# The products q·att of a linear attention as eight 64-row products in two row groups, instead of four 128-row products with zero blocks

## The reference

```python
xn = ln(x)
q = softmax((xn @ Wq + bq).reshape(b, t, h, 64), axis=-1)
k = softmax((xn @ Wk + bk + (1 - mask) * -1e6).reshape(b, t, h, 64), axis=1)
v = ((xn @ Wv + bv) * mask).reshape(b, t, h, 64)
att = einsum('bnhd,bnhl->bhdl', k, v)               # a 64 x 64 block for each head
y = einsum('bnhd,bhdl->bnhl', q, att)               # the products changed here
hh = ln(y) * (1 + scale) + shift                    # scale, shift from silu(emb) @ W_emb
out = x + silu(hh) @ W_out + b_out
```

## Time and profile before

| | us |
|---|---|
| median of 3 runs (510.15, 510.24, 513.07) | 510.24 |
| the profiled execution, its own time | 512.37 |
| its span in the profile | 510.5 |
| PE busy in the span | 471.0 |
| DVE busy | 365.2 |
| ACT busy | 264.6 |

### The profile page before, as it was taken

The page is one execution under the profiler, slowest core; times in us unless marked ns, Lnnn a source line. Parts: engine busy times, 40 slices in busy tenths (PEclk is TensorE's granted clock), DMA queues, the critical chain, the costliest instruction groups (busy, mean ns, idle before and its releaser), DMA issues.

```text
span 510.5 us, 7297 instructions
## 1 busy us (share of the span) xinstructions
PE 471.0 (92%) x2478; PEld 374.1 (73%) x2478; DVE 365.2 (72%) x893; ACT 264.6 (52%) x487; POOL 125.4 (25%) x106
## 2 busy tenths in 40 slices
PE   4998999999899989999999999998799979888987
PEld 2676776876688678878888888886578667676765
DVE  6699776686878747888685676759968348776643
ACT  4243333232787322355566555648898217366773
POOL 0013311120100001013343222344111201544655
PEclk9999999999999989999999999998999999999989
DMA  8991111111222211011121213211320001322444
GB/s 286 362 342 42 42 41 38 47 40 64 82 84 88 78 42 40 4 42 62 42 83 42 83 43 124 74 52 50 115 105 0 1 1 62 111 97 84 124 152 137
DMA packets 23093, 43.50 MB, mean 85 GB/s; under 512 B 1992, under 2 KB 2064, under 8 KB 23056
## 3 DMA queue, kind: packets, MB, share of 16 engines
q1 hardware_dynamic: 21968, 40.93, 23.8%
q10 hardware_dynamic: 1088, 2.10, 1.2%
HBM read 34.64 MB, written 8.39 MB: 84 GB/s over the span
## 4 chain that ended last, share of the span: by engine, by line
PE 69%; DVE 17%; ACT 6%; issue 5%; DMA 1%; POOL 0%; DVEq 0%; ACTq 0%
PE ps L1053 18%; PE ps L1055 17%; PE ps L1054 17%; PE ps L1058 8%; PE ps L1215 4%; PE ps L1146 1%; DVE xst_raw L611 1%; ACT ps L394 1%; DVE kf L810 1%; DVE qs L710 1%; DVE yst_raw L611 1%; ACT x_in L308 1%; DVE qmax L715 1%; DVE kf L746 1%; ACT kf L382 1%
## 5 line engine op out<-in xcount | busy, mean ns | idle before, releaser
L559 POOL TENSOR_TENSOR qs<-qs,qmax 128x512 f32<-128x512 f32 x32 | 35.2, 1099 | 203.1 <-DVE qmax L715 203.1
L1053 PE MATMUL ps<-wk_hi,zT_hi 128*128 128x512 f32 x128 | 54.3, 424 | 2.3 <-DVE kf L696 2.2
L1053 PE MATMUL ps<-ek_hi,zm_hi 128*128 128x512 f32 x128 | 50.8, 397 | 4.4 <-DVE ek_lo L751 3.7
L1053 PE MATMUL ps<-wq_hi,zT_hi 128*128 128x512 f32 x128 | 52.6, 411 | 0.3 <-DVE qs L710 0.3
L1054 PE MATMUL ps<-wk_lo,zT_hi 128*128 128x512 f32 x128 | 51.3, 401 | 0.0
L1055 PE MATMUL ps<-wk_hi,zT_lo 128*128 128x512 f32 x128 | 51.2, 400 | 0.0
L1055 PE MATMUL ps<-wq_hi,zT_lo 128*128 128x512 f32 x128 | 50.6, 395 | 0.0
L1054 PE MATMUL ps<-wq_lo,zT_hi 128*128 128x512 f32 x128 | 50.5, 395 | 0.0
L1055 PE MATMUL ps<-ek_hi,zm_lo 128*128 128x512 f32 x128 | 49.9, 390 | 0.0
L1054 PE MATMUL ps<-ek_lo,zm_hi 128*128 128x512 f32 x128 | 49.9, 390 | 0.0
L572 POOL TENSOR_TENSOR res<-res,bo_all 128x512 f32<-128x512 f32 x32 | 41.9, 1311 | 32.3 <-PE ps L1055 19.9
(11 more groups left out here) (210 smaller groups left out, 1158.8 us busy)
## 6 DMA issues: line engine op xcount, KB each, us to landing
x_in<-in_x_dram SPq DMA_DIRECT2D x32, 512.0 KB, 3.5
res<-in_x_dram SPq DMA_DIRECT2D x32, 256.0 KB, 2.8
out_dram<-res SPq DMA_DIRECT2D x32, 256.0 KB, 2.0
y<-in_L_cond_Wk_dram ACTq DMA_DIRECT2D x2, 512.0 KB, 5.0
kf<-in_L_cond_Wq_dram ACTq DMA_DIRECT2D x1, 1024.0 KB, 8.1
eq<-in_L_cond_W_out_dram SPq DMA_DIRECT2D x1, 1024.0 KB, 8.4
wv_mod<-in_L_cond_Wv_dram SPq DMA_DIRECT2D x1, 1024.0 KB, 10.6
eq<-in_L_cond_W_emb_dram SPq DMA_DIRECT2D x4, 256.0 KB, 10.1
```

What stands on the lines that cost most here:

```text
L559: pool.tensor_tensor(q_heads, q_heads, qmax[:].unsqueeze(2).broadcast_to([P, H, DH]), ALU.subtract).then_inc(s["q_shift"], 1)
L1053: pe.matmul(o, a[0], bb[0], start=start, stop=False)
```

## The change

`att` becomes 128 x 4 x 65: rows 0 to 63 hold the block of a pair's first head, rows 64 to 127 that of its second, and one column of ones serves both. A tile's four matmuls of 128 rows x 130 columns become eight of 64 rows x 65 columns. The two heads of a pair use the two halves of the array's rows and write to a bank each, at the same column offset, on all 128 output partitions. `products_att` issues the same matmuls and writes them more closely packed. `att_blocks` has one multiplication in place of two. The zero fill of `att` goes, and the memsets of ones are one in place of two. `y_tile` reads bank by bank (heads first, then pairs) and writes y in runs of 64 columns.

```diff
-    YW = P + 2
-    YS = 2 * P
+    YW = DH + 1
...
-                for h in range(2):
-                    r = slice(DH * h, DH * h + DH)
-                    dve.tensor_tensor(att[r, :, DH * h:DH * h + DH],
-                                      ps[r, YB + 1, :].rearrange("p (q h d) -> p q h d", q=NB, h=2)[:, :, h, :],
-                                      rz[r, :].unsqueeze(2).broadcast_to([DH, NB, DH]), ALU.mult).then_inc(s["att_step"], 1)
+                dve.tensor_tensor(att[:, :, 0:DH], ps[:, YB + 1, 0:NB * DH].rearrange("p (q d) -> p q d", d=DH),
+                                  rz[:].unsqueeze(2).broadcast_to([P, NB, DH]), ALU.mult).then_inc(s["att_step"], 1)
...
-                tile = ps[:, YB:YB + 2, :].rearrange("p k (q c) -> p (k q) c", c=YS)
-                rec_m = rec[:, m % 2, :].rearrange("p (q h) -> p q h", h=2)
+                tile = ps[:, YB:YB + 2, :].rearrange("p h (q c) -> p h q c", c=P)
+                rec_m = rec[:, m % 2, :].rearrange("p (h q) -> p h q", h=2)
...
-                dve.reciprocal(rec_m, tile[:, :, P:YW]).then_inc(s["y_rec"], 1)
+                dve.reciprocal(rec_m, tile[:, :, :, DH]).then_inc(s["y_rec"], 1)
...
-                dve.tensor_tensor(y_of(m).rearrange("p (q h d) -> p q h d", q=NB, h=2),
-                                  tile[:, :, 0:P].rearrange("p q (h d) -> p q h d", h=2),
-                                  rec_m.unsqueeze(3).broadcast_to([P, NB, 2, DH]), ALU.mult).then_inc(s["y_ok"], 1)
+                dve.tensor_tensor(y_of(m).rearrange("p (q h d) -> p h q d", q=NB, h=2), tile[:, :, :, 0:DH],
+                                  rec_m.unsqueeze(3).broadcast_to([P, 2, NB, DH]), ALU.mult).then_inc(s["y_ok"], 1)
...
-            dve.memset(att[:], 0.0).then_inc(s["att0"], 1)
+            dve.memset(att[:, :, DH:YW], 1.0).then_inc(s["att0"], 1)
...
-            dve.wait_ge(s["att0"], 1)
-            dve.memset(att[0:DH, :, P:P + 1], 1.0).then_inc(s["att0"], 1)
-            dve.memset(att[DH:P, :, P + 1:P + 2], 1.0).then_inc(s["att0"], 1)
...
-                            last = pe.matmul(ps[r, YB + 1, c], gT[:, f, c], wv_mod[:, f, c], start=(f == 0), stop=(f == NB - 1))
+                            last = pe.matmul(ps[r, YB + 1, q * DH:q * DH + DH], gT[:, f, c], wv_mod[:, f, c], start=(f == 0), stop=(f == NB - 1))
...
                 for q in range(NB):
-                    bank, at = YB + q // 2, (q % 2) * YS
-                    last = pe.matmul(ps[:, bank, at:at + YW], eqT[:, m % 2, q, :] if m < T else blk(eq[:, m - T, :], q),
-                                     att[:, q, :], start=True, stop=True)
+                    for h in range(2):
+                        r = slice(DH * h, DH * h + DH)
+                        last = pe.matmul(ps[:, YB + h, q * P:q * P + YW], turned[r, q, :], att[r, q, :], start=True, stop=True)
                 last.then_inc(s["y_ps"], 1)
```

More of the change, by code:

```diff
@@ L1209, in product_y @@
                 if m % T == 0:
-                    pe.wait_ge(s["att_step"], 2 * (m // T) + 2)
+                    pe.wait_ge(s["att_step"], m // T + 1)
                 if m:
                     pe.wait_ge(s["y_ok"], m)
+                turned = eqT[:, m % 2] if m < T else eq[:, m - T, :].rearrange("p (q c) -> p q c", c=P)
                 for q in range(NB):
-                    bank, at = YB + q // 2, (q % 2) * YS
-                    last = pe.matmul(ps[:, bank, at:at + YW], eqT[:, m % 2, q, :] if m < T else blk(eq[:, m - T, :], q),
-                                     att[:, q, :], start=True, stop=True)
+                    for h in range(2):
+                        r = slice(DH * h, DH * h + DH)
+                        last = pe.matmul(ps[:, YB + h, q * P:q * P + YW], turned[r, q, :], att[r, q, :], start=True, stop=True)
                 last.then_inc(s["y_ps"], 1)
@@ L1314, in _ @@
                 if t == 0:
-                    pe.wait_ge(s["att0"], 3)
+                    pe.wait_ge(s["att0"], 1)
                 product_y(t)
```

## The result

The changed kernel takes 519.34 us (median of 4 runs, 518.17 to 521.51), the kernel before 510.19 us beside it: a ratio of 1.0172, interval 1.0119 to 1.0226. It is slower by about 9 us, where 6.2 us was forecast. The sign, the size of the change-over (PE going over to 64 rows and back) and the pairs came out as forecast; of what is beyond them, 2.1 us at least are time at TensorE's lower clock, which the forecast didn't have.

What follows compares the result with a forecast made beforehand. PE was taken to bound the kernel, fully busy in the loop and waiting in turn with DVE and ACT in the tail. Loop 4.5 plus tail 1.7 gave +6.2 us, put on the median 510.24: 516.4 us, range 504 to 522.

Steps and rivals of the forecast that it cites:

- sign: Whole kernel: the change makes it slower, given a chance of 0.60; same 0.31, faster 0.09.
- change-over: Each call of the products of y: PE going to 64 rows and back costs 0.30 us, bounds 0.20 to 0.35.
- pairs: Products of y: sixteen loads run two at a time in the two row groups, keeping 0.89 us a call, 0 added.
- What bounds the kernel: Whole kernel: PE, busy 471.0 of 510.5 us; in the loop its gains or losses show in full.
- split of 0.20 going in: Each call: of the 0.30 us, about 0.20 is paid going into 64 rows and 0.10 coming out.
- The loop, +4.5 us: Tiles of the loop: 16 calls at 0.30 us make 4.8, less some absorbed by PE's waits in the first tiles.
- The tail, +1.7 us: Chain of waits in the tail: +0.4 us in its first tiles, then three periods of three tiles at 0.45, 1.35.
- the third call: Each three-tile period of the tail: off the chain, its 0.30 us covered by PE's 1.32 us wait for DVE.
- DVE and the memsets at 0: DVE's fewer multiplications, the dropped memsets and the multiplication into y in runs of 64: 0 us on the total.
- single file: Rival for the products of y: row groups don't overlap, a call costs 0.30 + 0.89 us more, 541 us; chance 0.14.
- No dry array: Rival for the products of y: no change-over needed, pairs run, loads stay the bound, about 0, 510 us; chance 0.12.
- Half loads: Rival for the products of y: 64-row loads take half the time, 505 us, chance 0.09; without change-over 498 us, 0.03.

Runs made afterwards that it cites:

- turned order: The changed kernel with its two inner loops swapped, four matmuls of one row group and then four of the other: 537.04 us beside 512.85 for the kernel before.
- full rows: The changed kernel with each of its eight matmuls on all 128 rows, the other head's rows of att being zeros: 538.09 us beside 512.85 for the kernel before.
- alone in the old kernel: The kernel before plus one unread matmul of 64 rows ahead of each product of y: 526.38 us; with 128 rows as control 517.13, beside 512.85.
- kernel with the loop alone: The new call of the products of y in tiles 0 to 15 only, the tail as in the kernel before: 515.05 us, ratio 1.0085.
- fillers: Matmuls whose result nobody reads, put into PE's waits; in the changed kernel at the start of the tail alone: 516.64 us, ratio 1.0086.
- tail alone: The new call of the products of y in tiles 16 to 31 only, the loop as in the kernel before: 515.11 us, ratio 1.0083.
- filled kernels: Changed kernel and kernel before with unread matmuls in PE's waits: 516.87 and 511.42 us at several places, 516.64 and 510.97 at the tail's start alone.
- first filled pair: Unread matmuls in PE's waits at the tail's start and three more places: changed kernel 516.87 us (ratio 1.0110), kernel before 511.42 (0.9998).

## Why the prediction was right, and where its sum was short

- **What bounds the kernel** held: PE was busy for all 115.00 us between 230 and 345 us, and what a call paid there showed in the tile's length.
- **Pairs, 0 us more for the matmuls** (part 1): right. The sixteen loads take 0.84 us in pairs of 0.11, and a load of 64 rows is as long as one of 128. The turned order shows what the alternation is worth, 0.5 us a call (11.83 us against 11.33). The full rows show what the row groups are worth to sixteen matmuls, their change-over paid: 0.55 (11.88).
- **The change-over, 0.30 us a call** (part 2): right in mechanism and size. In the changed kernel it is 11.33 - 11.05 = 0.28, alone in the old kernel 0.29. The split of 0.20 going in held too. One transposition of 64 rows at the start of the trace, was enough to price it. The Trainium skill's page "TensorEngine Tiling (Array Packing)" (Key Properties) says that a change of tiling mode drains the engine; the gap of 0.20 us ahead of each call agrees with it.
- **The loop, +4.5 us**: a little too much by the trace. From the first call to the last the changed kernel takes 341.73 - 190.78 = 150.95 us, before 340.03 - 192.60 = 147.43, so +3.5, and 0.3 for the last. Three of the first tiles paid almost nothing (0.01 to 0.02 us), since PE's waits took it up. I had set 0.3 us for that, and it was 0.9. The kernel with the loop alone measured +4.1.
- **The tail, +1.7 us**: this is the step that was mis-sized. The chain itself came out as worked out: a period of three tiles +0.48 for the forecast 0.45, the third call covered. With the clock kept up at its start, the whole tail, from the call of tile 16 to the end, is 98.42 us in the changed kernel and 96.48 in the kernel before, +1.9 us. But without fillers it is 100.97 in the changed kernel, of which 2.1 us lie between the calls of tiles 16 and 19 and 0.4 behind, where the changed kernel has its stretch at 493.7 us and the filled one none; and the tail alone measured +4.2. What failed is the silent assumption behind "I put it on the median", that the clock stays as it was. A call that starts from a wait was said to pay nothing or to gain 0.05; in fact the clock fell in these very calls. The fillers show that these waits and the clock are tied: with them 2.1 us go at this place, and 2.5 to 2.7 us of the whole by the medians (519.34 against 516.87 and 516.64). These medians stem from different comparisons, in which the kernel before took 510.2, 510.9 and 512.6 us, so the numbers of the traces are the firmer ones.
- **DVE and the memsets at 0**: right. The multiplication into y took 691 ns before and after. Without the memsets DVE waits 2.49 us for its first tile instead of 2.08, and starts it at 4.16 us instead of 4.25.
- **The sum**: the change-over costs 3.5 + 0.3 + 1.9 = 5.7 us by the traces, and 5.5 to 5.7 us lie between the medians of the filled kernels, for the forecast 6.2. The forecast called its 6.2 us a difference within the profiled execution, and there the difference is 6.0. That they agree so closely is luck: the changed kernel loses 2.5 us to the lower clock in the tail, the kernel before some 1.5 us at 184 us (8.03 us from the wait there to its first call, 6.57 in the changed kernel) and 0.5 in the tail (96.98 us against 96.48 filled), and these nearly cancel. Put on the median, the forecast fell 3 us short: the kernel before ran 2.2 us below its profiled execution by the median and the changed kernel 1.0 above. Runs of one and the same kernel differ in their mean clock, and their times with it (0.987 with 512.81 to 513.79 us, 0.996 with 509.4 to 510.56, for the kernel before beside the first filled pair), but which stretches these other runs had isn't shown. The whole, 519.34, is inside the range of 504 to 522, on its upper side.
- **The rivals**: single file is ruled out by the loads that start together. No dry array is ruled out by the 0.20 us ahead of each call. Half loads are ruled out by the 188 ns of a load of 64 rows, beside 191 for 128. The Trainium skill's page "TensorE: Matmul & The Clock Gate" (LDWEIGHTS) says that a load takes by its columns and not by its rows, and the trace agrees.

What stays open is why the clock falls there with the new calls and not with the old. PE's waits of 1.12 us are the same in both. It isn't the half as wide matmuls alone: the old calls with the extra matmul of 64 rows had 10.2 us at the lower level at that place, and with that of 128 rows none. But the full rows without any change-over had 6.8 us there too, from 431.9 us on, and the turned order 10.2. All of this is one profile a kernel, and the stretch at 184 us shows that the same wait can have one in one execution and none in another. For chance alone speaks little: all four runs of the changed kernel have a mean clock of 0.980 to 0.987, all six with fillers there 0.993 to 0.997. So I can say that with the waits filled the stretch is gone, and not what in the calls between them decides.

## What to carry to other kernels

Before splitting a matmul into row groups, read from the timeline what sets its pitch. Where it is the load of the stationary side, and that keeps its 128 columns, half the rows and half the moving columns are worth nothing, and each time over and back costs some 0.3 us. More products in a row in the same mode would spread that price, but no run here shows a gain that it could be set against. And where PE has short waits in a row, look at the granted clock after the change too: eight matmuls whose result nobody reads gave back 2.1 us at that place here.

## What the runs showed that I had not expected

- PE seems to look past the waiting row group: with one group's calls all ahead of the other's, a second stream of loads began 0.50 us after the first (272.42 against 271.92), with three of the first group's eight matmuls still to come, and the call took twelve steps and not sixteen.
- Going over to 64 rows and back costs as much for a single call of two columns (0.29 us) as for eight of 65 (0.28).
- The granted clock fell to 0.50 for 6.8 us while PE was busy for 9.71 of 12 us around it and never waited longer than 1.13 us. At 350.39 to 352.82 us a wait of 2.4 us stood shortly ahead of a stretch of 3.4 us, which began at 353.7.
